# The output sum of a fused FFN, Mamba and FFN kernel: from VectorE's additions to ScalarE's copies into and out of PSUM

## What is computed

```python
yh = (Y_diag + Y_off).reshape(b, l, H, P) + D_param[None, None, :, None] * x
hidden = yh.reshape(b, l, D_INNER) * silu(gate)          # D_INNER = 4096
var = mean(hidden * hidden, axis=-1)
hidden = hidden * rsqrt(var + EPS) * norm_w
x = x + hidden @ out_proj_w                              # 4096 -> 256
```

## Time and profile before

| | |
|---|---|
| median of three runs | 1468.12 us |
| the profiled execution, its time | 1469.74 us |
| its span in the profile | 1468.0 us |
| PE busy | 1336.6 us, 91% |
| DVE busy | 1190.8 us, 81% |
| ACT busy | 1007.1 us, 69% |
| POOL busy | 823.1 us, 56% |
| from 900 to 1000 us: PE, DVE, ACT, POOL | 97.49, 97.04, 85.67, 82.48 us |
| granted TensorE clock there | 1.00 of full speed |

### The profile page before, as it was taken

One profiled execution on the slowest core, in us unless ns is written; L12 is line 12 of the kernel. 1 busy time (PEld: TensorE's weight loads), 2 busy tenths in 40 slices (PEclk: granted clock), 3 DMA queues, 4 the chain that ended last, 5 costly groups with the idle time before them and its releaser, 6 DMA issues. The chain is left out here.

```text
span 1468.0 us, 27111 instructions
## 1 busy us (share of the span) xinstructions
PE 1336.6 (91%) x8896; PEld 1137.1 (77%) x8896; DVE 1190.8 (81%) x2643; ACT 1007.1 (69%) x2067; POOL 823.1 (56%) x896
## 2 busy tenths in 40 slices
PE   5889887767999999999999999999999999986998
PEld 4778776556888888888888888888888888864887
DVE  5753443576999999999999999999999999986433
ACT  1114433667889988888988898888899888861332
POOL 1004211004678787877878787797787878681000
PEclk9999987978999999999999999999999999995999
DMA  6221000223454554454564645644435544324000
GB/s 128 66 87 36 15 15 0 65 65 76 121 111 98 118 125 114 119 112 98 119 125 115 118 101 114 116 123 121 113 101 109 129 113 117 96 73 186 15 14 29
DMA packets 102085, 136.43 MB, mean 93 GB/s; under 512 B 27744, under 2 KB 49856, under 8 KB 101824
## 3 DMA queue, kind: packets, MB, share of 16 engines
q1 hardware_dynamic: 99840, 132.67, 37.6%
q10 hardware_dynamic: 2112, 2.10, 0.4%
HBM read 124.76 MB, written 9.96 MB: 92 GB/s over the span
## 5 line engine op out<-in xcount | busy, mean ns | idle before, releaser
L845 ACT ACTIVATE M<-cum_row,cum_table 128x128 f32<-128x128 f32 x1024 | 312.2, 390 | 0.0
L1240 DVE SCALAR_TENSOR_TENSOR xs<-psum,conv_w_sb,xs 128x509 f32<-128x509 f32 (+2 forms) x384 | 284.2, 740 | 0.4
L985 POOL TENSOR_TENSOR hid_lo<-hid,hid_hi 128x512 fp32r<-128x512 f32 x128 | 191.2, 1494 | 65.4 <-PE psum L40 59.6
L1028 POOL TENSOR_TENSOR hid<-hid,sg 128x512 f32<-128x512 f32 x128 | 165.7, 1295 | 89.5 <-DVE hid L1308 89.4
L1017 POOL TENSOR_TENSOR squares<-squares,sq 128x512 f32<-128x512 f32 x124 | 160.2, 1292 | 75.2 <-ACT sq L822 75.2
L1267 DVE TENSOR_TENSOR M<-M,CB 128x1024 f32<-128x1024 f32 x128 | 182.9, 1429 | 0.0
L1623 PE MATMUL psum<-M,xdt 128*64 128x128 f32 x2048 | 140.1, 279 | 20.8 <-DVE psum L1299 20.8
L827 ACT ACTIVATE sg<-psum 128x512 f32<-128x512 f32 x128 | 75.2, 587 | 102.2 <-PE psum L40 94.6
L1623 PEld LDWEIGHTS psum<-M,xdt 128*64 128x64 f32 x2048 | 109.9, 136 | 43.2 <-DVE M L1267 25.0
L1600 PE MATMUL psum<-xend,B_tok 128*128 128x128 f32 x1024 | 140.3, 281 | 2.1 <-DVE carry L1291 1.9
L859 ACT ACTIVATE xs<-psum,conv_b_sb,conv_w_sb 128x512 f32<-128x512 f32 x128 | 98.7, 771 | 52.7 <-PE psum L40 52.7
(11 more groups left out here) (210 smaller groups left out, 3432.5 us busy)
## 6 DMA issues: line engine op xcount, KB each, us to landing
cum_row<-cum_scratch SPq DMA_DIRECT2D x256, 256.0 KB, 4.6
e_row<-e_scratch SPq DMA_DIRECT2D x256, 128.0 KB, 3.5
xw_raw<-L_attn_in_proj_w_dram SPq DMA_DIRECT2D x32, 128.0 KB, 5.1
wo_raw<-L_attn_out_proj_w_dram SPq DMA_DIRECT2D x32, 128.0 KB, 4.6
gw_raw<-L_attn_in_proj_w_dram SPq DMA_DIRECT2D x16, 256.0 KB, 5.8
x_res<-_attn_hidden_states_dram ACTq DMA_DIRECT2D x4, 512.0 KB, 9.3
x_scratch<-x_res SPq DMA_DIRECT2D x4, 512.0 KB, 2.6
x_res<-x_scratch SPq DMA_DIRECT2D x1, 2048.0 KB, 7.6
```

The costliest lines, as they stand in the source:

```text
L845: last = nc.scalar.activation(M[:, v % 3, h, c * CH:(c + 1) * CH], cum_row[:, v % 2, h, c * CH:(c + 1) * CH], ACT.Relu, bias=scalar_of(CUM ...
L985: nc.gpsimd.tensor_tensor(hid_lo[:], hid[:, v % 2, :], hid_hi[:, v % 2, :].bitcast(F32), ALU.subtract).then_inc(hid_lo_done, 1)
L1028: nc.gpsimd.tensor_tensor(hid[:, v % 2, :], hid[:, v % 2, :], sg[:, v % 8, :], ALU.mult).then_inc(hid_done, 1)
L1240: nc.vector.scalar_tensor_tensor(xs[:, v % 7, shift:], psum[:, X_BANK + v % 2, 0:TT - shift], tap_of(v, step), xs[:, v % 7, shift:], ALU.m ...
```

## The change

It has three parts. (1) `add_out` goes from DVE. (2) ACT gets `take_out(s-1)` and `put_back(s)` behind `square(s)` in each phase slot: two copies of the banks into `mixed`, and, from the second group on (`v >= 16`), two copies of `mixed` of the tile that is next back into the banks, on which `out_proj` then accumulates without opening them (`start` is false, PE waits for `out_begun`). In the first group only the copies out are made. (3) On POOL `add_squares(s)` of the slots with `s % 4 == 1` goes from the slot's head behind `gate` and `split_hid` (and in u = 1 behind `split_wo` too).

```diff
+            def take_out(v):
+                t = at_slot(v)[1]
+                act.wait_ge(out_done, nth(v))
+                if v == GP - 1:
+                    act.wait_ge(cum_out, 16 * 2 * NT)
+                for m in range(KT):
+                    nc.scalar.activation(mixed[:, m, tile(t)], psum[:, OUT_BANK + m, :], ACT.Copy).then_inc(mixed_done, 1)
+
+            def put_back(v):
+                if not SLOTS <= v < ALL:
+                    return
+                t = at_slot(v)[1]
+                act.wait_ge(mixed_done, KT * (v // GP))
+                for m in range(KT):
+                    nc.scalar.activation(psum[:, OUT_BANK + m, :], mixed[:, m, tile(t)], ACT.Copy).then_inc(out_begun, 1)
...
             for s in range(-8, ALL):
                 if alive(s):
                     square(s)
+                if s > 0 and s % GP == 0:
+                    take_out(s - 1)
+                    put_back(s)
                 phase = s % GP == 0 and alive(s + 4)
...
+            take_out(ALL - 1)
...
             for s in range(-8, ALL):
-                if alive(s):
+                after_silu = s % GP == 1
+                if alive(s) and not after_silu:
                     add_squares(s)
...
                     split_wo(g * GP + GP - 1)
+                if alive(s) and after_silu:
+                    add_squares(s)
...
-            def add_out(v):
-                j, t = at_slot(v)
-                dve.wait_ge(out_done, nth(v))
-                if v == GP - 1:
-                    dve.wait_ge(cum_out, 16 * 2 * NT)
-                for m in range(KT):
-                    if v < SLOTS:
-                        nc.vector.tensor_copy(mixed[:, m, tile(t)], psum[:, OUT_BANK + m, :]).then_inc(mixed_done, 1)
-                    else:
-                        nc.vector.tensor_tensor(mixed[:, m, tile(t)], psum[:, OUT_BANK + m, :], mixed[:, m, tile(t)],
-                                                ALU.add).then_inc(mixed_done, 1)
...
-                if s >= 0 and s % GP == GP - 1:
-                    add_out(s)
...
                 if j == 0:
                     pe.wait_ge(mixed_done, KT * (v // GP))
+                    if v >= SLOTS:
+                        pe.wait_ge(out_begun, KT * (v // GP - NT + 1))
                 for m in range(KT):
...
-                                        hid_hi[:, v % 2, :], hid_lo[:], start=(j == 0), stop=(j == GP - 1))
+                                        hid_hi[:, v % 2, :], hid_lo[:], start=(j == 0 and v < SLOTS),
+                                        stop=(j == GP - 1), skip=(v >= SLOTS))
```

More of the change, by code:

```diff
@@ L470, in macaron @@
     halo_in, halo_step, halo_done = sem("halo_in"), sem("halo_step"), sem("halo_done")
-    folded = sem("folded")
+    folded, out_begun = sem("folded"), sem("out_begun")
     wo_hi_done, wo_lo_done, hid_hi_done, hid_lo_done = [sem(n) for n in ("wo_hi_done", "wo_lo_done", "hid_hi_done", "hid_lo_done")]
```

## The result

The kernel after takes 1492.88 us (median of five runs, 1484.45 to 1493.34) against 1468.12 us (five runs, 1466.21 to 1471.08). Over all the runs the ratio is 1.0148, 95% interval 1.012 to 1.0177; the two medians alone give 1.0169, since the median of the five runs after lies near the upper end of their spread. Slower was right, and the time lies 5.9 us over the forecast. The profiled execution of the kernel after is the fastest of its five, 1484.45 us (span 1482.7 us).

The account below looks back on a forecast made before the run. PE was taken to run almost without a pause, with some 4.4 us of stops a group. 3.1 us more a group (18.6 in six), 1.3 in the last, less 1.5, gave +18.4: 1487 us, range 1473 to 1502.

Parts of the forecast that it names:

- The shift on ACT: On ACT ahead of the phase slot's table load: four copies make later work 2.1 us later, bounds 1.0 and 3.0 us.
- C: Rival, faster: copies back cost little or ACT is early, so DVE does not wait for evac_x; 1457 or 1450 us, chance 0.12.
- D: Rival, slower still: copies into PSUM on ACT cost 1 us each; 1505 us, chance 0.09.
- The chain: Behind the phase slot: late evac_x delays DVE's head, hid_lo locks M out for 0.73 us, PE stops some 1.75 us.
- T: The time of the head of a phase slot (u = 4, 8, 12, 0) on PE's timeline.
- The stretches from T to T: PE's four stretches of four slots a group: 0.5, 0.1, 1.75 and 0.75 us longer from u = 4, 8, 12, 0.
- The sum: Whole kernel: 3.1 us a group, 18.6 in six full groups, 1.3 in the last, 0 in the first, +18.4 us in all.
- The 1.5 saved in the last slots: In the last slots, where DVE sets the pace, the additions that go save 1.5 us.
- The stop in the third slot: PE's stop for L1299 moves from the slot behind the phase slot to the third one and lasts 1.7 to 1.9 us.
- I cost it at nothing: On POOL: the squares' move ends the wait for ACT's square, up to 3.8 us; a later square makes hid late, priced zero.
- B: Rival, late evacuation but M not locked out by hid_lo: 1.65 us a group, about +9 us, 1477 us, chance 0.18.
- E: Rival, no change: one stop replaces another at the same price, or margins were misjudged; 1468 us, chance 0.06.

Follow-up runs that it names:

- the execution of 1491.67 us: The kernel after, unchanged, profiled once more: 1491.67 us, span 1490.0 us.
- copies out alone: The kernel after without the two copies back into the banks and the wait for them: 1462.14 us, ratio 0.9964.
- gates first: The kernel after with POOL splitting the gate weights before the squares in u = 9: 1479.87 us, ratio 1.0077.
- all orders: The kernel after with ACT's evacuations before the relus, gate weights before squares in u = 9, squares before out weights in u = 1: 1448.16 us.
- the two orders made in the kernel before: The kernel before, additions kept on DVE, once with ACT's evacuations before the relus (1470.21 us), once with all four changed orders on ACT and POOL (1471.53 us).
- back twice: The kernel after with two more copies of the same values into the banks ahead of the two that count: 1526.64 us, ratio 1.0406.
- evacuation first: The kernel after with ACT's two evacuations before the eight relus in the slot behind the phase slot: 1463.97 us, 0.997 times the kernel before.
- M first: The kernel after with POOL's hid_lo waiting for DVE's M times CB in the second slot behind each phase slot: 1480.17 us, ratio 1.0085.
- part 3 alone: The kernel before with only the squares moved last on POOL in the slots behind a phase slot: 1481.65 us, ratio 1.0089.
- squares first: The kernel after with POOL's old order, add_squares at the head of every slot: 1511.97 us, ratio 1.0304.

## Why the prediction held, step by step

- **The shift on ACT, 2.1 us.** Measured 2.19 less the overlap. The copy back averages 593 ns, the copy out 588, and the silu within SBUF, the row it was priced by, 620. The Trainium skill ("ScalarE: Activation LUTs", What happens when an `exp` ACTIVATE runs) has ScalarE writing PSUM with less delay than SBUF. One copy back is indeed 27 ns shorter than one silu within SBUF (another function, so this is not shown to be the destination), but the next one starts 0.53 us after it, as in the silu batch ((2.20 - 0.62) / 3). So a pair back takes the predicted 1.12 us, and the rule did not carry it to C's side. What starts sooner is the copy that reads PSUM, 0.48 us after the one before. D's price of 1 us each is refuted by the same rows.
- **The chain.** Evacuation at T + 17.7 predicted, 17.75 measured; `diag` from u = 4, 12 and 0 at T + 26.0, 25.8 and 25.7 predicted, 25.98, 25.74 and 25.55 measured; M locked out for 0.73, shown by taking the lock away. That lock is the one of the Trainium skill ("SBUF — State Buffer", Who interferes with whom): M takes 1.95 us beside hid_lo and 1.22 when hid_lo is made to wait for it.
- **The stretches from T to T** (PE's L1610): u = 4: 32.14 (predicted 32.2), u = 8: 32.27 (32.55), u = 12: 31.70 (31.7), u = 0: 31.74 (31.8). Together 127.85, 2.7 more a group where 3.1 was forecast (2.8 by the cut at `diag`). From u = 0 M was free (1.22 us at 870.63), as forecast.
- **The sum.** Loop: 6 x 2.8 = 16.7 (18.6 forecast), first group -1.5 (0 forecast: it gained 1.2 from v = 4 and 0.3 from v = 8, and lost nothing from v = 12), last group +1.2 and -1.1 (+1.3 and -1.5), 0.25 in the second group. These are 15.5; the other 3.1 of the measured 18.6 are two falls of the clock, which the sum did not have. That the loop comes out at the forecast's 18.4 is in part luck. The 1.5 saved in the last slots are not there as a whole either: 1.1 are won before the last `diag`, and behind it PE stops 1.42 us for the copies back.
- **The stop in the third slot.** Forecast as one of 1.7 to 1.9 us for L1299. From u = 4 it is split: 0.51 for the scan and 0.91 for the scaled PSUM, 1.42 us of idle rows; `diag` is 25.98 - 24.25 = 1.73 us late, as forecast.
- **POOL.** "I cost it at nothing" was right only for this sum. Part 3 is no free edit: by itself it costs 13.5 us, on top of parts 1 and 2 it saves 19. The number held because the squares had been counted in the chain to gw_lo (PE was to start at T + 19.8, it started at 19.54). The reason given did not hold: "hid is not what PE waits for" leaves out that POOL makes gw_lo behind hid, so with the squares first the late hid reaches PE as a stop of 3.8 us.
- **The rivals.** B: M is locked. C: true at a shift of 1.05 us, by the run with the copies out alone (1462 us, forecast 1457). E: refuted by the interval.
- **What was missing:** the 5.9 us by which the median is above the forecast. The profiled execution lies 8.4 us below the median, and below the 1488 that the sum gave for it; it came to the loop 5.7 us sooner, with a higher granted clock (0.91 against 0.79, from 180 to 240 us). In the execution of 1491.67 us, near the median, two further clock falls (3.1 us) and 4.0 us more ahead of the loop, with a granted clock of 0.84 there, make up the difference to the profiled one. Falls of the clock were not in the sum; what sets the clock at these places was not tried.

## What to carry to other kernels

When work is moved from a busy engine to an idler one, price it where it lands: not by that engine's busy share but by the first result behind it for which another engine is about to ask. Here 2.1 us ahead of a batch met a reserve of 0.75 us (1.6 us with DVE's own lateness), and beyond it a microsecond on ACT cost about one of kernel time, in part by the locks that the lateness let in; moving two instructions of the receiving engine ahead of ones that nobody awaits made a loss of 25 us a gain of 4, and the same two moved in the kernel before gained nothing: the sum had to be off DVE for that. And a reordering on a third engine must be tried with and without the rest: the same edit cost 13.5 us alone and saved 19 in company.

## What the runs showed of the hardware that was not expected

In some groups TensorE's granted clock fell behind the stop of 1.8 us for gw_lo. Two places of the same execution, 4 us each, with the same stop (columns: length, busy time and count on PE, PEclk, DMA share, GB/s):

```profile
673.00:677.00 4.00, 3.83 (x10) 0.58 0.78 163
802.00:806.00 4.00, 3.40 (x15) 1.00 0.85 164
```

```profile
673.79 0.63 PE L40 MATMUL psum<-xT_hi,gw_lo 128*128 128x512 f32 x1
...
803.17 0.39 PE L40 MATMUL psum<-xT_hi,gw_lo 128*128 128x512 f32 x1
```

In the first the clock is partly at its lower level of 1.2 GHz, and a matmul takes 0.63 us for 0.39. Each such place makes the stretch 33.85 us instead of 32.28, 1.57 us. It came in 2, 4 and 2 of 7 groups of the three profiled executions of the kernel after. All runs together, one place in each of seven groups of an execution, by the length of PE's stop for gw_lo there:

| stop, us | kernels | places | clock fell in |
|---|---|---|---|
| 0.43 to 0.83 | before, gates first, all orders, the two orders made in the kernel before | 35 | 0 |
| 1.24, 2.3 us behind a stop of 0.9 | back twice | 6 | 2 |
| 1.64 to 1.67 | copies out alone; the first group of six others | 13 | 0 |
| 1.78 to 1.81 | after (three times), evacuation first, M first | 30 | 12 |
| 2.02 to 2.05 | part 3 alone | 7 | 1 |
| 2.95 to 3.83 | squares first | 7 | 7 |

So the length of the stop alone does not decide it between 1.2 and 2.1 us: the same kernel at the same place went either way. At 3 us and more the clock fell every time, at 0.8 us and less never. What decides in between was not tried.
